# Cross-attention and feed-forward on one core: the attention's residual and output bias added in DRAM by accumulating transfers

## The reference, cut to what matters

```python
def _L0_xattn_ref(query, key_value, Wq, bq, Wk, bk, Wv, bv, Wo, bo):
    ...
    attn = softmax(clip(q @ k.T * scale, -CLAMP, CLAMP))     # 16 heads of 32 channels, 64 keys
    attn = where(any(isnan(attn)), 1.0 / Nkv, attn)          # one test over the whole attention
    x = (attn @ v).reshape(B, Nq, Cq)
    return x @ Wo + bo
...
x = x + _L0_xattn_ref(_layernorm(x), ctx_768, Wq, bq, Wk, bk, Wv, bv, Wo, bo)   # this sum is called x1 below
x = x + _L0_ffn_ref(_layernorm(x), W1, b1, phases, w_real, w_imag, W2, b2)
```

## Time and profile before

| | |
|---|---|
| time, median of 3 runs | 1963.59 us (1960.86 to 1963.77) |
| the profiled execution's own time | 1960.05 us |
| its span, first to last instruction | 1958.0 us |
| mean granted TensorE clock | 0.999 |
| attention, until PE's first feed-forward chunk | 0 to 630 us of the span |
| feed-forward | 630 to 1958 us |

### The profile page before, as it was taken

One profiled execution on the slowest core, in us unless ns is written; L12 is line 12 of the kernel. 1 busy time (PEld: TensorE's weight loads), 2 busy tenths in 40 slices (PEclk: granted clock), 3 DMA queues, 4 the chain that ended last, 5 costly groups with the idle time before them and its releaser, 6 DMA issues.

```text
span 1958.0 us, 27871 instructions
## 1 busy us (share of the span) xinstructions
PE 1940.6 (99%) x9162; PEld 1622.7 (83%) x9162; DVE 1493.0 (76%) x2308; ACT 1263.5 (65%) x2132; POOL 549.9 (28%) x391
## 2 busy tenths in 40 slices
PE   9999999999999999999999999999999999999999
PEld 7788888888888788788888888888888888888887
DVE  8988888888876986787578768758757876875763
ACT  6767767667664877577377557647737755764761
POOL 7877777777775321000000000000000000000000
PEclk9999999999999999999999999999999999999999
DMA  7456565566544999899899898998989989898845
GB/s 245 143 163 163 153 166 156 150 176 165 146 116 146 335 347 306 257 297 290 275 309 270 264 311 264 285 278 292 289 278 305 268 267 310 265 283 246 251 151 193
DMA packets 361186, 468.55 MB, mean 239 GB/s; under 512 B 165968, under 2 KB 201808, under 8 KB 361040
## 3 DMA queue, kind: packets, MB, share of 16 engines
q1 hardware_dynamic: 346448, 439.44, 71.0%
q0 software_dynamic: 13728, 27.26, 7.6%
q10 hardware_dynamic: 864, 0.04, 0.0%
HBM read 347.90 MB, written 91.23 MB: 224 GB/s over the span
## 4 chain that ended last, share of the span: by engine, by line
PE 89%; DVE 4%; ACT 2%; DMA 2%; POOL 2%; issue 1%; SPq 0%; POOLq 0%; ACTq 0%; DVEq 0%
PE psum L1999 29%; PE psum L2001 29%; PE psum L2000 29%; PE psum L2092 3%; DMA w_ring<-w1s 1%; DMA x_dram<-res 0%; POOL prob L946 0%; POOL prob L967 0%; DVE stats L1493 0%; DVE top L1629 0%; DVE prob L1620 0%; DVE acc L1846 0%; DVE xt_lo L1729 0%; POOL sums L541 0%; DMA x_sb<-in_x 0%
## 5 line engine op out<-in xcount | busy, mean ns | idle before, releaser
L1999 PE MATMUL psum<-w_ring,act_hi 128*128 128x512 f32 x1024 | 398.7, 389 | 1.6 <-DVE act_lo L1831 1.5
L2000 PE MATMUL psum<-w_ring,act_hi 128*128 128x512 f32 x1024 | 398.4, 389 | 0.0
L2001 PE MATMUL psum<-w_ring,act_lo 128*128 128x512 f32 x1024 | 398.4, 389 | 0.0
L1999 PE MATMUL psum<-xo,w_ring 128*128 128x512 f32 x784 | 305.8, 390 | 2.8 <-ACT p_sb L1365 2.5
L2000 PE MATMUL psum<-xo,w_ring 128*128 128x512 f32 x784 | 305.5, 390 | 0.0
L2001 PE MATMUL psum<-xo,w_ring 128*128 128x512 f32 x784 | 305.5, 390 | 0.0
L1810 DVE SCALAR_TENSOR_TENSOR frac<-frac,turns 128x512 f32<-128x512 f32 x256 | 174.5, 691 | 79.6 <-ACT frac L1358 79.6
L1999 PEld LDWEIGHTS psum<-w_ring,act_hi 128*128 128x128 f32 x1024 | 192.3, 188 | 43.2 <-issue 3.4
L2001 PEld LDWEIGHTS psum<-w_ring,act_lo 128*128 128x128 f32 x1024 | 192.3, 188 | 40.0
L2000 PEld LDWEIGHTS psum<-w_ring,act_hi 128*128 128x128 f32 x1024 | 192.3, 188 | 39.6
L1395 ACT ACTIVATE frac<-frac 128x512 f32<-128x512 f32 x256 | 156.1, 626 | 104.4 <-DVE frac L1810 104.4
(11 more groups left out here) (190 smaller groups left out, 4349.8 us busy)
## 6 DMA issues: line engine op xcount, KB each, us to landing
w_ring<-w2s SPq DMA_DIRECT2D x240, 512.0 KB, 4.3
w_ring<-w1s SPq DMA_DIRECT2D x392, 256.0 KB, 6.1
x_sb<-turn_dram SPq DMA_DIRECT2D x58, 512.0 KB, 6.7
res<-in_x SPq DMA_DIRECT2D x64, 256.0 KB, 3.9
x_dram<-res SPq DMA_DIRECT2D x64, 256.0 KB, 3.1
acc<-x_dram SPq DMA_DIRECT2D x16, 1024.0 KB, 7.6
x_sb<-in_x SPq DMA_DIRECT2D x15, 1024.0 KB, 6.3
x_sb<-x_dram SPq DMA_DIRECT2D x15, 1024.0 KB, 7.9
```

The source lines that it names most:

```text
L1999: pe.matmul(o, a_hi, b_hi, start=first, stop=False, skip_group_check=resumed)
L2000: pe.matmul(o, a_hi, b_lo, start=False, stop=False, skip_group_check=resumed)
L2001: return pe.matmul(o, a_lo, b_hi, start=False, stop=last, skip_group_check=resumed)
```

## The change

ACT's new `output_row` copies the block of y from PSUM to `res`, in the same step as PE's product, between the exponential and the copy of `o_hi`; DVE adds nothing, and x is not loaded into `res`. SP stores the block as before. POOL then issues two transfers per tile that add in DRAM: `add_input_rows` adds the tile of x to `x1_dram`, and `add_bias_rows` adds `bo_row`. In the loop POOL issues the first for tile t at the end of its step i = 11 + 4t, the second at the end of step 13 + 4t. The bias of tile 13 comes after the loop, ahead of the wait for `nan_count`. Tiles 14 and 15 come between the two branches, ahead of `last_done`. The additions of `bo` where x1 is read back go away.

```diff
-        def output_row(i):                      # VectorE
-            if 0 <= n < TILES * NB:
-                dve.wait_ge(res_in[n % NB], 16 * (n // NB + 1))
-                dve.wait_ge(y_psum, n + 1)
-                dve.tensor_tensor(res[:, n % NB, :], psum[:, y_bank(i), :], res[:, n % NB, :], ALU.add)
+            def output_row(i):                  # ScalarE
+                if 0 <= n < TILES * NB:
+                    act.wait_ge(y_psum, n + 1)
+                    if n < NB:
+                        act.wait_ge(w_lo_done, 2 * KC)
+                    else:
+                        act.wait_ge(x1_stored[n % NB], 16 * (n // NB))
+                    act.activation(res[:, n % NB, :], psum[:, y_bank(i), :], ACT.Copy).then_inc(y_done, 1)
...
+            def add_input_rows(t):
+                if t:
+                    pool.wait_ge(x1_summed, 16 * t)
+                for blk in range(NB):
+                    pool.wait_ge(x1_stored[blk], 16 * (t + 1))
+                pool.dma_start(x1_rows[t], x_rows[t], accum_op=ALU.add).then_inc(x1_summed, 16)
+
+            def add_bias_rows(t):
+                pool.wait_ge(x1_summed, 16 * (t + 1))
+                if t:
+                    pool.wait_ge(x1_biased, 16 * t)
+                pool.dma_start(x1_rows[t], bo_row[:].unsqueeze(1).to_broadcast([P, NB, C]), accum_op=ALU.add)\
+                    .then_inc(x1_biased, 16)
...
+                if biased_tile(i) is not None:          # i = 11 + 4t
+                    add_input_rows(biased_tile(i))
+                if biased_tile(i - 2) is not None:
+                    add_bias_rows(biased_tile(i - 2))
...
+            add_bias_rows(GUARDED - 1)
             pool.wait_ge(nan_count, 4)
...
             pool.memset(ones[:], 1.0).then_inc(guard_done, 1)
-            for n in range(NB):
-                add_first_bias(n)
             rsqrt(TILES)
-            pool.wait_ge(shift_rows_done, TILES + 1)
-            for half in range(2):
-                add_row_bias(1, half)
+            for t in range(GUARDED, TILES):
+                add_input_rows(t)
+                add_bias_rows(t)
...
             pool.memset(ones[:], 1.0).then_inc(last_done, 1)
...
             for T in range(1, FFN_PAIRS):
-                if more:
-                    add_row_bias_by_dma(2 * T + 2)
                 add_last_bias_by_dma(2 * T)
...
+                sp.wait_ge(x1_biased, 16 * (T + 1))     # ahead of every later load of x1 rows
```

More of the change, by code:

```diff
@@ L409, in half_rows, with biased_tile @@
             return slice(part * NB // 2, (part + 1) * NB // 2)
+        def biased_tile(i):
+            t, late = divmod(i - LAG_A - 2 * KC - 1, KC)
+            return t if t >= 0 and not late else None
         def by_pair(row):
@@ L1007, in uniform @@
                 added(pool.tensor_tensor(tile, tile, u_row.unsqueeze(1).to_broadcast([P, tile.shape[1], C]), ALU.add))
+                added(pool.tensor_tensor(tile, tile, bo_row[:].unsqueeze(1).to_broadcast([P, tile.shape[1], C]), ALU.add))
                 for blk in range(tile.shape[1]):
@@ L1091, in _ @@
                 mean_outputs()
-                for blk in range(NB):
-                    pool.wait_ge(x1_stored[blk], 16 * GUARDED)
+                pool.wait_ge(x1_biased, 16 * GUARDED)
                 for t in range(GUARDED):
@@ L1120, in _ @@
                     pool.wait_ge(b2_in, 16)
-                    pool.tensor_tensor(b2_row[:], b2_row[:], bo_row[:], ALU.add).then_inc(b2_biased, 1)
-                    pool.wait_ge(b2_biased, 1)
                 if pair_summed(j) is not None:
@@ L1128, in _ @@
                     rsqrt(TILES + 3)
-            def add_row_bias_by_dma(T):
-                pool.wait_ge(x_in[T % 2], x_loads(TILES + T))
-                pool.dma_start(x_sb[T % 2][:], bo_row[:].unsqueeze(1).to_broadcast([P, NB, C]), accum_op=ALU.add)\
-                    .then_inc(rows_added[T % 2], 16)
             def add_last_bias_by_dma(T):
@@ L1291, in _ @@
                     layer_rows(1, range(NB))
+                output_row(i)
                 if late >= 0:
@@ L1302, in _ @@
                         act.activation(wo_hi[:, k, :], res[:, k, :], ACT.Copy).then_inc(w_hi_done, 1)
+            for i in range(GROUPS + LAG_A, STEPS_A - 2):
+                output_row(i)
             act.wait_ge(par_step, PAR_REDUCED + 4)
@@ L1308, in _ @@
             layer_rows(TILES, range(NB))
+            for i in range(STEPS_A - 2, STEPS_A):
+                output_row(i)
             act.wait_ge(q_psum, GROUPS)
@@ L1637, in pt_to_lo @@
                                           ALU.subtract).then_inc(pt_lo_done, 1)
-            def output_row(i):
-                n = i - LAG_A - KC
-                if 0 <= n < TILES * NB:
-                    dve.wait_ge(res_in[n % NB], 16 * (n // NB + 1))
-                    dve.wait_ge(y_psum, n + 1)
-                    dve.tensor_tensor(res[:, n % NB, :], psum[:, y_bank(i), :], res[:, n % NB, :], ALU.add)\
-                        .then_inc(y_done, 1)
             for i in range(STEPS_A):
@@ L1846, in add_outputs @@
                     dve.tensor_tensor(rows, psum[:, Y2_BANK + n, :], rows, ALU.add).then_inc(y2_done, 1)
-            def add_row_bias(T, half):
-                dve.wait_ge(x_in[T % 2], x_loads(TILES + T))
-                rows = x_sb[T % 2][:, half_rows(half), :]
-                dve.tensor_tensor(rows, rows, bo_row[:].unsqueeze(1).to_broadcast([P, NB // 2, C]), ALU.add)\
-                    .then_inc(x1_whole, 1)
             def add_last_bias(T, half):
```

41 lines of the change are left out of this document (12 added, 29 removed).

## The result

| | before | after |
|---|---|---|
| median | 1963.32 us, 4 runs (1960.86 to 1963.77) | 1997.27 us, 4 runs (1995.30 to 1999.74) |
| ratio | | 1.0178, 95% interval 1.0165 to 1.0190: 1.8% slower, clear of the noise |
| the profiled execution and its span | 1960.05, 1958.0 us | 1997.48, 1995.3 us |

The change costs 34 us between the medians and 37.3 between the two profiled spans: the execution profiled before lies 3.3 us under its kernel's median, the one after 0.2 us above its own. The traces are compared on spans.

The account below looks back on a forecast made before the run. PE, 99% busy, was taken as the bound. Terms 29.1 + 2.6 + 1.3 + 1.5 - 0.5 = 34.0 us on the profiled 1960.05 gave 1994; with the median's 3.5 us, 1997. Range 1983 to 2010, chance 0.60.

Parts of the forecast that it names:

- bias issues in steady attention: Steady attention: POOL's bias issue delays `q_lo`, PE waits 0.2 us for each of 13 tiles, 2.6 us; bounds 0 and 10.
- the passage, release of ACT: Attention to feed-forward: POOL's three waits for landings release ACT, DVE and SP at 664.2 instead of 635.1, +29.1 us.
- half clock, and chunk loads late: After PE's stall: seven matmuls at half clock, 1.3 us (1 to 3); next chunk loads late, 1.5 us (0 to 6.3).
- feed-forward lighter: Feed-forward: 12 transfers into `x_sb` and four DVE adds go away, gaining 0.5 us.
- What bounds the kernel: Whole kernel: PE is 99% busy, so freeing DVE or transfers gains at most its 17 us idle; delays cost their whole length.
- ACT's copy at nothing: Steady attention: ACT's 0.6 us copy mostly fits before its next input exists, cost nothing; bound above 9 us.
- over 20 us idle ahead of second 0: Sign in the changed profile: PE idle for over 20 us ahead of the first matmul of feed-forward second 0.
- The offset of 3.5 us: Whole time: the runs' median lies 3.5 us above the profiled execution, added to 1994 to put 1997.
- 1: Passage: added transfers land like plain ones, 6.3 us each, release +8.6, time 1976; chance 0.14 (up to 1983).
- 2: Adding in DRAM is slower than in SBUF (passage +48, about 2017), or steady steps lose more; chance 0.20 (above 2010).
- 3: Passage: not slower, waits for landing end before block 63 has landed anyway, some 1961 us; chance 0.04.

Follow-up runs that it names:

- experiment 8: Experiment 7's first kernel with late additions issued one by one, none at a pair's turn: 1962.00 us against 1961.79 before the change; control without those six: 1961.17.
- experiment 4: Changed kernel with ACT's output copy behind `o_hi` instead of ahead of it in every fourth step: 1997.24 us, ratio 1.0179.
- experiment 6: Against a 1981.11 us kernel (late additions between POOL's sums, each bias issued with the next tile's input), DVE instead of ACT copies output rows: 1985.02 us.
- experiment 7: Changed kernel, biases of tiles 12 to 15 and inputs of 14, 15 moved into the feed-forward pair loop: 1980.23 us with experiment 3's order, 1986.46 with the change's.
- experiment 3: Changed kernel with each tile's bias issued in attention together with the next tile's input, four steps behind its own, not two: 1991.36 us, ratio 1.0154.
- experiment 1: Changed kernel with the additions of tiles 14 and 15 issued after `last_done` instead of before it: 1992.22 us, ratio 1.0153.
- experiment 2: Experiment 1's kernel with the bias of tile 13 also added after the guard: 1994.99 us, ratio 1.0171.

## Why the prediction was right, and where its terms were off

The forecast was 1997 and the median is 1997.27. The mechanism held; the terms less so:

| term | predicted | in the trace |
|---|---|---|
| bias issues in steady attention | 2.6 (0 to 10) | 12.1 at POOL's last shift, 0.7 of it there before the first addition; when undone alone 6.2 between medians, 7.9 in the traces |
| the passage, release of ACT | 29.1 | 24.2 (36.3 less 12.1) |
| half clock, and chunk loads late | 1.3 and 1.5 | 1.6 together by 846 us (37.8 less PE's 36.2 at second 0) |
| feed-forward lighter | -0.5 | -0.5 (37.3 less 37.8) |
| sum | 34.0 | 37.3 between spans, 34.0 between medians |

- **What bounds the kernel.** Right. The loss of PE's time was never made up, and experiment 8 shows that DVE's and ACT's changed load together was worth nothing.
- **ACT's copy at nothing.** Right: 579 ns each (median), no wait of PE on it, and experiments 4 and 6 moved it without gain.
- **The bias issue in attention.** Mis-sized: the push of 1.3 us on POOL was right, but only PE's direct wait for `q_lo` was followed. The pushed `q_lo` met DVE's `xt_lo` a tenth of a microsecond later, so that `halves` got ahead of the fourth of them; the four grew from 3.17 to 4.38 us, and the delay came back to POOL through DVE's tops. That gave up to 1.3 us for a tile, not 0.2. The row bound of 10 us was just too low for the trace (12.1), while the amount that undoing it gave back lies inside.
- **The passage.** Each link was there in the order written. Landings in DRAM took 9.9, 10.6 and 13.8 us (with POOL's next issue at their end) where 11.4, 12 and 15 had been taken from transfers into SBUF; block 59 landed 14.6 us behind the guard, 13.5 forecast. Another term was too long: wait, register load and branch behind the count were put at 3.4 us, as before, but the count had long been ready, and the guard was set 1.9 us behind the end of the bias issue. With 0.5 us by which two issues overlap, these differences make up the 4.9 us that 29.1 is above 24.2. The sign "over 20 us idle ahead of second 0" did not come out as written: PE stood 17.0 us there, and 6.6 more ahead of the first rows, which the working had only as a later start of the first chunk.
- **The clock.** Fourteen matmuls at half the clock, not seven (14 x 0.2 = 2.8 us), and ACT waited 3.08 and 1.19 us for chunks behind the bias of 15, which cost PE 1.5 us from one matmul's start to the next at 687. The kernel before lost 2.6 us in the same stretch, counted in the same way, around waits of 0.74 and 0.73 us that are absorbed now. That leaves about 1.6 us net: the sum of two terms near what was written, by other parts.
- **The offset of 3.5 us** between median and profiled execution was added to the new kernel as well. The new profiled execution lies on its median. This error and the one of 3.4 us in the sum cancelled. Inside the sum, too, attention was 9.5 us too low and the passage 4.9 too high. That the total came out within a microsecond is luck.
- **The rivals.** 1: landings came between a plain load's 6.3 and the forecast's, so its direction had something, its size didn't. 2: steady steps did lose more, but not by longer issues: POOL's 16 bias issues took 1.32 us at most, so the 3.1 us that the Trainium skill's page "SBUF — State Buffer", section "SBUF: two separate sides", gives for a transfer that DVE holds up (one of 0.62 us alone, so not the time of an issue, as the prediction took it) does not show here. Whether any DVE instruction beside these issues ran in the mode that the page names, the rows don't say. 3: no.

Landings after the change (KB each, median us), against the earlier trace rows:

```profile
x_dram<-in_x POOLq DMA_DIRECT2D x16, 1024.0 KB, 9.6
x_dram<-bo_row POOLq DMA_DIRECT2D x16, 1024.0 KB, 10.9
```

The estimate of 4.4 us by the Trainium skill's page "DMA: Bandwidth & Descriptors", section "Anatomy of one DMA — SWDGE (gpsimd) path", is contradicted by both rows for accumulating transfers from a broadcast row and from DRAM alike.

The 12.1 us at the end of attention and the 6.2 us between medians go together so. In the traces of experiment 7 POOL's last shift is at 615.44 with the change's order and at 607.51 with experiment 3's, 7.9 us apart, and PE's wait for `p_sb` is at 818.80 and 810.87, again 7.9. The other 4.5 us at the last shift stay with experiment 3's order too; 2.3 of them are the step of 11.4 us with the double issue. In both kernels 2.2 us of what had come down from attention are absorbed by 811 us. The medians differ by less than the traces, and the five runs of the first kernel spread over 6 us.

What stays open: why the same 4.38 us on DVE, which stand there for every tile from 160 us on, lengthen a step by 1.2 us in the first half of attention and by 0.5 in the second; and why experiment 6 is 4 us slower.

## What to carry to other kernels

A wait for a landing costs all the work that stands behind it in the engine's queue, not only what needs the landing: moving the mark ahead of the wait (experiments 1 and 2) only hands the stall to the next work in the queue, and it goes away when each wait is put where its landing is long over. Then look at the stretch into which the transfer has been moved: six transfers of 1 MB cost some 18 us where they were issued ahead of loads that the bound engine needs, up to three at once, and nothing when issued one by one in other places. For an engine that is 99% busy, ask of every push of a microsecond on a neighbour which operations it will now run beside and which of the two will start first, not only who waits for the pushed one.

## What the runs showed of the hardware

- DVE's `xt_lo` (two operands in SBUF, 128x512) took 0.68 us alone, and 1.77 when it started 0.05 us behind POOL's `halves` (1.28 us). Where it started 0.07 us ahead, it took 0.68 and `halves` 1.75. Four in a row took 4.38 us in the first case and 3.17 in the second. In the kernel before DVE was first by 0.06 us: 0.68 and 1.76.
- POOL's instruction behind a DMA issue took 1.80 us instead of 1.30 (`halves` at 414.51), while the issue's record of 1.31 us overlaps it by 0.5.
- An accumulating transfer of 1 MB into DRAM landed in 8.5 to 13.1 us (median 10.3) after the change, in 13.4 to 16.1 for the input when issued together with a bias (experiment 8, attention), and in 19.8 and 27.3 as second and third ahead of two row loads. Those into SBUF had 11.4 at least.
- The added writes, 91.23 to 124.78 MB, cost by themselves nothing that 11 runs can show (experiment 8, whose page has the same 124.78 MB).
